# Evacuating the slot in front directly behind silu on ScalarE, in the expert slots of a gated cross-attention and mixture-of-experts layer

## The reference

```
x = x + tanh(g_xattn) * attention(layernorm(x), ctx)      # 32 heads of 128, 4 key/value heads, keys: ctx and x
x = x + tanh(g_ffn)   * ffn(layernorm(x))
```

```
scores = softmax(xt @ router_w + router_b) + router_bias      # best 2 of 4 groups, then best 2 experts
h = silu(xt @ w1 + b1) * (xt @ w2 + b2)                       # per expert
y = y + gate * (h @ w3 + b3)
z = silu(xt @ sw1 + sb1) * (xt @ sw2 + sb2) @ sw3 + sb3       # the shared expert
return y + z
```

## Time and profile before

| what | value |
|---|---|
| median of 3 runs | 1545.6 us (1543.26 to 1545.85) |
| the profiled execution, its own time | 1544.32 us |
| its span in the profile | 1542.6 us |
| granted TensorE clock, mean share of full speed | 0.987 |
| PE busy, share of the span | 95% |
| DVE busy | 63% |
| ACT busy | 50% |
| POOL busy | 12% |

### The profile page before, as it was taken

How to read it: one execution, slowest core, us unless ns; L and a number is a source line. 1 busy time by engine, 2 the same in 40 slices (tenths; PEclk the granted TensorE clock), 3 DMA queues, 4 the chain that set the end, 5 groups by cost and what they waited for, 6 DMA issues and landing times.

```text
span 1542.6 us, 26300 instructions
## 1 busy us (share of the span) xinstructions
PE 1470.0 (95%) x9136; PEld 1306.0 (85%) x9136; DVE 973.8 (63%) x1632; ACT 779.0 (50%) x2028; POOL 188.0 (12%) x198
## 2 busy tenths in 40 slices
PE   7999988999999999999999999999999999888986
PEld 5888878999999999989999989999998778887874
DVE  5322237666677666666766657776666778666657
ACT  3112216555566555555655546555555545676760
POOL 0000000000000000000000000000003423677750
PEclk9999999999999999999999999999999999999998
DMA  7576542111223111132211122221110303677528
GB/s 233 162 228 168 138 163 96 48 63 54 68 76 109 64 42 48 66 107 69 74 50 69 41 70 76 82 90 42 48 49 15 110 29 110 226 239 251 162 83 327
DMA packets 97447, 163.67 MB, mean 106 GB/s; under 512 B 12435, under 2 KB 47287, under 8 KB 93258
## 3 DMA queue, kind: packets, MB, share of 16 engines
q1 hardware_dynamic: 87370, 145.62, 29.0%
q0 software_dynamic: 9984, 16.82, 3.3%
HBM read 128.29 MB, written 49.81 MB: 115 GB/s over the span
## 4 chain that ended last, share of the span: by engine, by line
PE 69%; issue 6%; DVE 4%; ACT 2%; SPq 2%; DMA 1%; another core or an unknown queue 1%; ACTq 0%; DVEq 0%
PE ps_q L84 8%; PE ps_q L86 8%; PE ps_q L85 8%; PE ps_y L85 8%; PE ps_y L84 8%; PE ps_y L86 8%; PE ps_s L1008 5%; PE ps_p L1048 4%; PE ps_o L84 2%; PE ps_s L1010 2%; PE ps_o L86 2%; PE ps_o L85 2%; PE bank L84 1%; PE bank L86 1%; PE bank L85 1%
## 5 line engine op out<-in xcount | busy, mean ns | idle before, releaser
L84 PE MATMUL ps_q<-xt,wq_hi 128*128 128x256 f32 x1024 | 302.6, 295 | 4.4 <-PEq L118 4.4
L86 PE MATMUL ps_q<-xt,wq_hi 128*128 128x256 f32 x1024 | 291.7, 285 | 0.0
L85 PE MATMUL ps_q<-xt,wq_lo 128*128 128x256 f32 x1024 | 291.7, 285 | 0.0
L842 ACT ACTIVATE s_sb<-s_sb,nmax 128x128 f32<-128x128 f32 x512 | 199.9, 392 | 129.7 <-DVE nmax L924 129.7
L922 DVE TENSOR_TENSOR s_sb<-ps_s,s_cross 128x512 f32<-128x512 f32 x128 | 88.4, 691 | 232.4 <-ACT s_cross L831 232.2
L831 ACT ACTIVATE s_cross<-ps_s 128x512 f32<-128x512 f32 x128 | 76.5, 597 | 272.3 <-PE ps_s L1010 272.3
L84 PE MATMUL ps_y<-wo_hi,o_hi 128*128 128x512 f32 x512 | 202.3, 395 | 0.9 <-DVE y L902 0.9
L86 PE MATMUL ps_y<-wo_lo,o_hi 128*128 128x512 f32 x512 | 202.6, 396 | 0.0
L85 PE MATMUL ps_y<-wo_hi,o_lo 128*128 128x512 f32 x512 | 202.6, 396 | 0.0
L84 PEld LDWEIGHTS ps_q<-xt,wq_hi 128*128 128x128 f32 x1024 | 196.9, 192 | 5.0 <-issue 4.8
L85 PEld LDWEIGHTS ps_q<-xt,wq_lo 128*128 128x128 f32 x1024 | 197.1, 193 | 0.0
(11 more groups left out here) (262 smaller groups left out, 3230.3 us busy)
## 6 DMA issues: line engine op xcount, KB each, us to landing
xt<-x_scratch SPq DMA_DIRECT2D x32, 1024.0 KB, 4.9
w_raw<-in_L_ffn_ew SPq DMA_DIRECT2D x93, 256.0 KB
v_full<-v_out SPq DMA_DIRECT2D x64, 128.0 KB, 2.6
k_full<-k_out SPq DMA_DIRECT2D x16, 512.0 KB, 2.8
w_raw<-in_L_xattn_Wq SPq DMA_DIRECT2D x16, 512.0 KB, 5.1
kt_raw<-k_full SPq DMA_DIRECT2D x32, 256.0 KB, 2.6
vt_raw<-v_full SPq DMA_DIRECT2D x32, 256.0 KB, 2.7
w_raw<-in_L_xattn_Wo SPq DMA_DIRECT2D x16, 512.0 KB, 4.3
```

The source lines that it names most:

```text
L84: pe.matmul(out, w_hi, x_hi, start=first, stop=False)
L85: pe.matmul(out, w_lo, x_hi, start=False, stop=False)
L86: return pe.matmul(out, w_hi, x_lo, start=False, stop=last)
L842: last = act.activation(s_sb[:, i], s_sb[:, i], ACT.Exp, bias=nmax[:, i:i + 1], accum_out=sums[:, i:i + 1])
```

## The change

In ScalarE's slot, evacuate(s - 1, 1 - r) moves from behind h_hi to directly behind silu. Buffers, semaphores, loads and all other queues stay as they are.

```
                 act.activation(silu[r], ps_up[r][:, 0], ACT.Silu, bias=biases[r][:, 0:1]).then_inc(silu_made, 1)
+                if late(s, 1):
+                    evacuate(s - 1, 1 - r)
 
                 act.wait_ge(h_made, s + 1)
                 if late(s, 2):
                     act.wait_ge(down_done, 2 * s - 2)
                 act.activation(h_hi[r], h_sb[r], ACT.Copy).then_inc(h_hi_made, 1)
-                if late(s, 1):
-                    evacuate(s - 1, 1 - r)
                 if not (isinstance(s, int) and s == LAST):
                     w_down_high(s + 1, 1 - r)
```

## The result

| | before | changed |
|---|---|---|
| median of 20 runs each | 1545.6 us | 1549.6 us |
| ratio, 95% interval | | 1.0024 [1.0013, 1.0036] |
| span of the profiled execution | 1542.6 us | 1546.8 us |
| first silu to last silu | 1311.4 to 1497.4 (186.0 us) | 1310.9 to 1500.8 (189.9 us) |
| behind the last silu | 45.2 us | 46.0 us |

A forecast was written before the change was run, and what follows sets the result against it. The slots were taken to be bound by a chain through several engines, 6.26 us each, none full. Terms 4.1 + 1.0 + 1.1 - 0.87 = 5.3 us gained, from 1545.6 to 1540.3 us; range 1534.5 to 1547.5.

The forecast's parts named there:

- The steps behind silu: ScalarE per slot: w_hi (down) 2.24 us behind late silu instead of 2.64, 1.14 sooner between; last h_hi 1.9 to 2.0.
- 0.87: Last slot: h_hi comes 0.87 us later with nothing to hide it, a loss; bounds 0.44 and 1.54.
- The term of the last slots: From silu of slot 28 none is late, so one pair leaves the path: 1.1 us gained, bounds 0 and 1.14.
- the first term of the sum: 12 slots with late silu: w_hi (down) 0.40 us sooner in 11, 0.30 lost in one; 4.1 us gained.
- What is late next there is TensorE's signal for silu, so I cost this at 0: Slots between late ones: w_hi (down) 1.14 us sooner, a 0.51 load wait goes; counted as no gain.
- the first slots' 1.0: Slots before late signals begin: weight load comes about 1.0 us sooner, shortening a 1.62 us wait; 1.0 gained.
- B: Before silu: TensorE's signal keeps its own pace, earlier ScalarE work becomes longer remote wait; no change, 1545; chance 0.31.
- C: Behind silu: ScalarE waits for down's second half with h_hi queued behind; 4.7 us lost, 1550.3; chance 0.09.
- A's test: In late slots, w_hi (down) stays at 1.86 us behind silu, down's signals being there with silu.
- A: 12 late slots: down's signals are there with silu, each gives 0.78 us; 10.6 gained, 1535.0; chance 0.13.

The follow-up runs named there:

- sitting 1: The prediction's own measurement on one chip: kernel before 1545.6 us, changed kernel 1549.6 us, ratio 1.0024; late signals present.
- g2: Old order with TensorE's up signal put off, sent by the turn of the slot after the next, against the kernel before: 1570.75 us, ratio 1.0162.
- g3: New order with TensorE's up signal put off in the same way, against the kernel before: 1559.62 us, ratio 1.0066.
- sitting 3: Both kernels run again unchanged, beside two edits with delayed weight loads: kernel before 1535.1 us, ratio of the change 0.9975; no late signals.
- sitting 7: One more pair of both kernels unchanged: kernel before 1534.76 us, changed 1529.02 us, ratio 0.9962; no late signals.
- f2: The changed kernel, unchanged, run again against the kernel before: 1530.03 us, ratio 0.9975.
- e1: Two kernels, POOL's gathers and scatters replaced by plain DMAs from SP, against the kernel before: old order 1536.85 us (1.0010), new order 1530.58 us (0.9973).
- h2: Old order with POOL's indirect DMAs replaced by plain ones from SP, repeated, against the kernel before at 1547.16 us: 1535.78 us, ratio 0.9926.
- h3: New order with POOL's indirect DMAs replaced by plain ones from SP, repeated, against the kernel before at 1547.16 us: 1529.50 us, ratio 0.9882.
- h4: The kernel before, unchanged, traced on a chip with late signals: 1547.30 us, ratio 0.9998.
- g1: The changed kernel, unchanged, run again against the kernel before at 1547.88 us: 1555.66 us, ratio 1.0046.
- h1: New order with SP's weight load delayed behind the first xs_lo of the next slot, repeated, against the kernel before at 1547.16 us: 1556.78 us, ratio 1.0049.
- i1: Old order, POOL's scatter of slot s also waiting for up of slot s + 2, against the kernel before at 1535.76 us: 1576.05 us, ratio 1.0256.
- i2: New order, POOL's scatter of slot s also waiting for up of slot s + 2, against the kernel before at 1535.76 us: 1567.13 us, ratio 1.0212.
- sittings 1, 4 and 5: The three with late signals: the prediction's own, the one with signals put off, and the repeat without POOL's indirect DMAs; kernel before 1545.6, 1547.88, 1547.16 us.
- sitting 6: Both orders with POOL's scatters held back, against the kernel before at 1535.76 us: ratios 1.0256 (old order) and 1.0212 (new order).
- e2: New order with SP's weight load of slot s waiting for the first xs_lo of slot s - 1, against the kernel before: 1533.26 us, ratio 0.9984.
- f1: The kernel before, unchanged, run again for its trace: 1536.25 us, ratio 1.0008.
- f3: Old order with SP's weight load delayed behind the first xs_lo of the next slot, against the kernel before: 1542.10 us, ratio 1.0041.
- j1: The changed kernel, unchanged, in one more pair against the kernel before at 1534.76 us: 1529.02 us, ratio 0.9962.
- sitting 2: First follow-ups, on plain DMAs, delayed loads and earlier down weights, against the kernel before at 1535.7 us: ratios 0.9973 to 1.0041; no late signals.
- sitting 5: Delayed loads and plain DMAs repeated, kernel before at 1547.16 us: ratios 1.0049 (delayed loads), 0.9926 and 0.9882 (plain DMAs, old and new order).

## Why the prediction was wrong

**The steps behind silu were right.** w_hi (down) in late slots at 2.31 (forecast 2.24; the mean of slots from 1.82 to 3.06), in the slots between 1.1 us sooner, the last h_hi at 1.97 (1.9 to 2.0), and 0.8 us more behind the last silu (0.87). The term of the last slots can't be read here: from silu of 28 to silu of 30 it was 10.66 us and is 8.94, but silu of 28 is now itself released late, where the prediction had none late from 28 on, and that shortens the interval; from silu of 26 to silu of 30 it is 21.7 us and was 21.6.

**The step that failed** is the first term of the sum, for the slots with a silu that is released late, "11 x 0.40 - 0.30 = 4.1 us gained". It held TensorE's lateness at 2.5 us while ScalarE's work, and POOL's behind it, moved forward. In sitting 1 the lateness grew, from a mean of 2.7 us in 12 slots to 3.4 in 14, and silu's unassigned wait with it by 14.0 us. Two slots, for which 12.0 us were forecast, took 12.7 on the mean (12.4 before). The same goes for "What is late next there is TensorE's signal for silu, so I cost this at 0", and for the first slots' 1.0. In the changed kernel's ScalarE timeline the 1.62 us wait of the earlier trace rows is shorter, and silu behind it waits instead:

```profile
1326.12 1.06 ACT L1702 ACTIVATE w_hi<-w_raw 128x1024 fp32r<-128x1024 f32 x1 [0.95 <-issue]
1330.03 0.47 ACT L1728 ACTIVATE silu<-bank,biases 128x256 f32<-128x256 f32 x1 [2.85 <-remote]
```

Silu of slot 3 starts 0.7 us later than before, at 1330.03 instead of 1329.33, where 1.0 sooner was forecast. g2 and g3 show that ScalarE's order is worth something where the lateness is set by hand, about 0.4 us a slot. That this equals the term's 0.40 is no proof of its working: there down's signals are there with silu, for which the prediction had 0.78.

**The rivals.** B had the place right (the wait in front of silu grows), but let it grow only by what was saved: 14 x (2.64 - 2.31) = 4.6 us, and it grew by 14.0. C's 1550.3 is the nearest number, by luck: C's mechanism, down's second half held up behind silu, is seen in 4 of 14 late slots (w_hi at 2.97 to 3.06), and is not where the time went. A's test, w_hi at 1.86, came true in six of the 14 late slots (1.82) without A's gain.

**What the prediction couldn't see** is that the profile of before shows one of two conditions that a sitting can be in. Without late signals ScalarE bounds every slot, not 12 of 31, and the change gains 5.1 us in sitting 3 and 5.7 in sitting 7, by another way than the sum's: 0.34 us in each of 30 steps in the traced executions, less 0.9 behind the last. That this is near the forecast's 5.3 is chance.

The sittings without late signals show how far a signal lies from the recorded end by itself: all of the 119 signals of f2 between 1345 and 1480 us come 0.013 to 0.015 us behind it. The 2.5 us of the earlier trace rows were something else.

**What stays open.** Late signals were seen only with POOL's indirect DMAs (without them 0 of 455, in e1's two kernels, h2 and h3), only in the slots, and only in some sittings. What differs between those sittings isn't known, nor by what path POOL's work could hold a signal up. That the new order makes them later is measured (a mean of 2.7 and 3.4 us in sitting 1; 2.6 to 2.7 in most late slots of h4 and 3.7 to 5.2 in most of g1 and h1), that the earlier scatters do it is argued from POOL's rows and not shown; i1 and i2 fell in a sitting that couldn't tell. Nor was it looked into whether the events that are missing from the same traces have the same cause, or whether TensorE's work itself ended later than its records say: the ends are modelled.

No version tried beats the changed kernel in the sittings without late signals, nor the kernel before in those with them, short of taking the indirect DMAs off POOL.

## What to carry to other kernels

When an engine waits on a signal that comes microseconds behind the record of the work that sends it, don't reckon other edits against this wait as a constant: here its mean went from 2.7 us to 3.4 with the edit, and in two of four sittings no signal was late. Find first what it hangs on, and whether it is there in another sitting. Repeat the kernel before in more than one sitting before a change of a few tenths of a per cent is judged; here 20 runs in one sitting gave a clear interval with the wrong sign for two of the four sittings that had both kernels. And an order change that fills an engine's idle time is worth what the next waits leave of it: 1.1 us saved per slot became 0.34.

## What the runs showed of the hardware

- In sittings 1, 4 and 5 about half of TensorE's semaphore signals in the slots, where POOL issues indirect DMAs, came 1 to 5 us behind the recorded end (61 of 108 in the kernel before of sitting 1, 48 of 94 in g1). In sitting 6, on the chip of g1, none did (0 of 84 in i1, 0 of 90 in i2). The kernel before takes 1545.6 to 1547.9 us in the one case and 1534.8 to 1535.8 in the other.
- In the sittings with late signals, 53 of the 57 up signals that found an indirect DMA on POOL 0.25 us or more under way were late, and 4 of the other 46. In the traces of e2, f1, f2, f3 and j1, without late signals, the same overlap delayed nothing (0 of 82).
- The traces with late signals also lack events of semaphores (silu's: 22 of 31 before, 15 of 31 after, all 31 in f1 and f2).
- Four plain DMAs of the same size a slot from SP, in place of POOL's two gathers and two scatters, left the old order where it was in sitting 2 (1.0010) and gained 0.7% in sitting 5 (0.9926), where the kernel before has late signals.
- In the kernel before of sitting 1 POOL is busy for about 1.0 us with one indirect DMA of 128 rows of 2 KB (medians: 1.04 a gather, 0.99 the second scatter, 1.35 the first; the longest gather 1.70) and 0.3 until the next. The added wait in front of the scatters (i1, i2) held up the gathers queued behind: TensorE's wait for rows was 45.9 and 38.5 us against 5.1 in f1, and the kernels took 40 and 31 us more than the kernel before, where at most 0.3% was expected.
